# Transposes, Gram products and a running maximum, reordered in the opening of a one-core language-model block

## The reference

```
h = rms_norm(rms_norm(emb[x], nw) @ projT, None)            # 2 x 1024 x 512
h = h + attention(layernorm(h), wq, wk, wv, wo)             # causal softmax(q k' / 4) v
h = h + (silu(n @ w_gate.T) * (n @ w_up.T)) @ w_down.T      # n = layernorm(h)
```

## Time and profile before

| | |
|---|---|
| median of 3 executions | 723.34 us (723.07 to 725.62) |
| the profiled execution | 722.81 us |
| its span, first to last instruction | 721.0 us |
| instructions | 16350 |
| TensorE busy | 693.3 us (96%) |
| VectorE busy | 414.4 us (57%) |
| ScalarE busy | 334.5 us (46%) |
| GpSimd busy | 295.6 us (41%) |

### The profile page before, as it was taken

The page is one execution under the profiler, slowest core; times in us unless marked ns, Lnnn a source line. Parts: engine busy times, 40 slices in busy tenths (PEclk is TensorE's granted clock), DMA queues, the critical chain, the costliest instruction groups (busy, mean ns, idle before and its releaser), DMA issues.

```text
span 721.0 us, 16350 instructions
## 1 busy us (share of the span) xinstructions
PE 693.3 (96%) x6399; PEld 530.2 (74%) x6399; DVE 414.4 (57%) x1041; ACT 334.5 (46%) x691; POOL 295.6 (41%) x398
## 2 busy tenths in 40 slices
PE   8459989999999999999999999999999999999998
PEld 5359679974898569965997489856996499847873
DVE  7867789885654556554655465555655365543320
ACT  6426368862565226631665046622674066512320
POOL 5020212241365426752565436642665246611220
PEclk9859999999999999999999999999999999999999
DMA  8759410011000110002000210012000300000000
GB/s 319 306 196 401 150 40 2 2 28 63 33 2 1 61 61 2 2 17 97 9 2 2 69 54 3 1 47 76 2 2 1 107 15 2 1 16 15 2 1 29
DMA packets 10459, 40.37 MB, mean 56 GB/s; under 512 B 1808, under 2 KB 2576, under 8 KB 8592
## 3 DMA queue, kind: packets, MB, share of 16 engines
q1 hardware_dynamic: 6912, 25.44, 9.1%
q0 software_dynamic: 3328, 13.11, 5.7%
q10 hardware_dynamic: 144, 0.79, 0.3%
HBM read 29.89 MB, written 9.44 MB: 55 GB/s over the span
## 4 chain that ended last, share of the span: by engine, by line
PE 88%; DVE 8%; ACT 2%; issue 1%; POOL 1%; DVEq 0%; POOLq 0%; ACTq 0%
PE banks L1106 15%; PE banks L1108 15%; PE banks L1107 15%; PE banks L1197 6%; PE banks L1199 6%; PE banks L1198 6%; PE banks L1060 4%; PE banks L1078 3%; PE banks L1049 2%; PE banks L1142 2%; PE banks L1144 2%; PE banks L1143 2%; PE banks L1084 1%; PE banks L1038 1%; PE banks L1085 1%
## 5 line engine op out<-in xcount | busy, mean ns | idle before, releaser
L1108 PE MATMUL banks<-xnT_and_h,ffn_weights 128*128 128x256 f16 x1024 | 279.0, 272 | 0.0
L1106 PE MATMUL banks<-xnT_and_h,ffn_weights 128*128 128x256 f16 x1024 | 278.8, 272 | 0.1
L1107 PE MATMUL banks<-xnT_and_h,ffn_weights 128*128 128x256 f16 x1024 | 278.9, 272 | 0.0
L374 POOL TENSOR_TENSOR gated_split<-gate_work,gated_split 128x256 f16<-128x256 f32 x128 | 86.7, 678 | 260.6 <-ACT gated_split L518 260.6
L378 POOL TENSOR_TENSOR weights_split<-weights,weights_split 128x512 f16<-128x512 f32 x96 | 111.3, 1159 | 0.0
L1106 PEld LDWEIGHTS banks<-xnT_and_h,ffn_weights 128*128 128x128 f16 x1024 | 101.0, 99 | 11.9 <-DVE xnT_and_h L878 0.6
L1108 PEld LDWEIGHTS banks<-xnT_and_h,ffn_weights 128*128 128x128 f16 x1024 | 100.0, 98 | 11.8
L1107 PEld LDWEIGHTS banks<-xnT_and_h,ffn_weights 128*128 128x128 f16 x1024 | 99.9, 98 | 11.2
L506 ACT ACTIVATE gate_work<-banks,scales 128x256 f32<-128x256 f32 x128 | 60.7, 474 | 99.8 <-PE banks L1108 99.7
L828 DVE SCALAR_TENSOR_TENSOR weights<-weights,counts_T 128x512 f32<-128x512 f32 x128 | 87.8, 686 | 11.6 <-ACT weights L514 11.5
L514 ACT ACTIVATE weights<-banks,scales 128x512 f32<-128x512 f32 x128 | 87.3, 682 | 14.5 <-PE banks L1060 14.5
(11 more groups left out here) (232 smaller groups left out, 1063.9 us busy)
## 6 DMA issues: line engine op xcount, KB each, us to landing
ffn_weights<-in_ffn_w SPq DMA_DIRECT2D x12, 1024.0 KB, 11.2
out_rows_dram<-ffn_weights SPq DMA_DIRECT2D x16, 256.0 KB, 2.0
xnT_and_h<-in_wqkv SPq DMA_DIRECT2D x1, 1536.0 KB, 8.6
local_table<-gated_split SPq DMA_DIRECT2D x2, 640.0 KB, 4.4
local_table<-xnT_and_h SPq DMA_DIRECT2D x2, 640.0 KB, 6.0
gated_split<-in_projT SPq DMA_DIRECT2D x4, 256.0 KB, 4.0
ffn_weights<-in_wo SPq DMA_DIRECT2D x1, 1024.0 KB, 10.6
token_table<-weights_split ACTq DMA_DIRECT2D x1, 768.0 KB, 5.2
```

The lines of the kernel that those rows point to most:

```text
L374: g.tensor_tensor(gtl[:, j, :], g2[j % 2], gth[:, j, :], ALU.subtract).then_inc(gt_lo, 1)
L1106: t.matmul(o, wh, xTh[m % 2][:, c, :], start=c == 0, stop=False)
L1107: t.matmul(o, wh, xTl[m % 2][:, c, :], start=False, stop=False)
L1108: last = t.matmul(o, wl, xTh[m % 2][:, c, :], start=False, stop=c == DC - 1)
```

## The change

- VectorE computes the indices and ranks ahead of the QKV scales, and the permutation ahead of the low part of Q.
- TensorE makes the key tables ahead of the transposes of K.
- Each key table is copied out in two halves of 512 columns, the first by ScalarE, the second by VectorE. ScalarE waits for `kn` first, then copies its two halves and KstA; VectorE copies KstB after its own halves.
- The prefix over the eight groups is made by doubling: a memset and three maxima, then one, then one more, with a scratch tile of 256 columns. For sequence 1 it moves from slots 0 to 7 into slots 3 to 5.
- Of the Gram products six come before `turn(0)` and six after it, where 16 came before it; 14 are in slot 0 (20 before), 12 in slot 1, and nine in each of slots 2 to 11 (eight before).

```diff
-GU_LEAD = 16
-GU_GRAM = {0: (16, 36), 1: (36, 48), **{s: (32 + 8 * s, 40 + 8 * s) for s in range(2, 12)}}
+GU_LEAD = (6, 12)
+GU_GRAM = {0: (12, 26), 1: (26, 38), **{s: (20 + 9 * s, 29 + 9 * s) for s in range(2, 12)}}
-GROUP_SLOTS = range(0, 8)
+GROUP_SLOTS = range(3, 6)
...
+        gtwo = agth[:, 5 * BLK:6 * BLK]
...
             actq.wait_ge(tab["kn"], 1)
+            for b in range(B):
+                actq.wait_ge(tab["kb"], b + 1)
+                a.activation(Kb[b][:, 0:512], bank[2 - 2 * b], ACT.Copy).then_inc(tab["kb_ev_act"], 1)
             a.activation(KstA[0:64, :], bank16[5][0:64, :], ACT.Copy).then_inc(tab["kn_ev"], 1)
-            actq.wait_ge(tab["kn_ev"], 1)
-            a.activation(KstB[64:128, :], bank16[5][64:128, :], ACT.Copy).then_inc(tab["kn_ev"], 1)
...
-            dve.wait_ge(tab["qkv_sum"], 1)
-            root_powers(POWQ, bank[2][:, 0:3], 3)
-            link(v.tensor_scalar(sc[:, 8:11], sc[:, 60:63], QKV_UP, None, ALU.mult))
-            v.tensor_scalar(sc[:, 16:19], sc[:, 8:11], st[:, 24:25], None, ALU.mult).then_inc(tab["cols"], 1)
-            v.tensor_scalar(c_exp, pw(POWQ), pw(POWQ + 1), 0.25 / QKV_UP ** 2, ALU.mult, ALU.mult)
...
             link(v.tensor_reduce(t_rank, t_cmp.rearrange("p (b u) -> p b u", b=B), AX.X, ALU.add))
+            dve.wait_ge(tab["qkv_sum"], 1)
+            root_powers(POWQ, bank[2][:, 0:3], 3)
+            link(v.tensor_scalar(sc[:, 8:11], sc[:, 60:63], QKV_UP, None, ALU.mult))
+            v.tensor_scalar(sc[:, 16:19], sc[:, 8:11], st[:, 24:25], None, ALU.mult).then_inc(tab["cols"], 1)
+            v.tensor_scalar(c_exp, pw(POWQ), pw(POWQ + 1), 0.25 / QKV_UP ** 2, ALU.mult, ALU.mult)
+
+            for b in range(B):
+                v.tensor_scalar(t_perm[:, b * P:(b + 1) * P], t_iota_r, t_rank[:, b:b + 1], None, ALU.is_equal).then_inc(tab["perm"], 1)
+
             qt = t_q.rearrange("p (h c d) -> p h c d", h=HEADS, d=HD)
             q3 = bank[7].rearrange("p (h d) -> p h d", d=HD)
             dve.wait_ge(tab["qh"], 1)
             v.scalar_tensor_tensor(qt[:, :, 2, :], q3, r_q, qt[:, :, 0, :], ALU.mult, ALU.subtract).then_inc(tab["qlow"], 1)
-            for b in range(B):
-                v.tensor_scalar(t_perm[:, b * P:(b + 1) * P], t_iota_r, t_rank[:, b:b + 1], None, ALU.is_equal).then_inc(tab["perm"], 1)
...
-            def key_table(b):
-                o = (1 - b) * 1024
-                dve.wait_ge(tab["kb"], b + 1)
-                v.tensor_copy(Kb[b], ps[:, o:o + 1024]).then_inc(tab["kb_ev"], 1)
-
             dve.wait_ge(tab["qT"], 2)
             v.tensor_copy(t_QT[:, 1024:2048], bank16[7]).then_inc(tab["qT_ev"], 1)
-            key_table(0)
-            key_table(1)
+            for b in range(B):
+                dve.wait_ge(tab["kb"], b + 1)
+                v.tensor_copy(Kb[b][:, 512:1024], bank[3 - 2 * b]).then_inc(tab["kb_ev"], 1)
+            dve.wait_ge(tab["kn"], 1)
+            dve.wait_ge(tab["zeroed"], 4)
+            v.tensor_copy(KstB[64:128, :], bank16[5][64:128, :]).then_inc(tab["kn_ev"], 1)
...
-            def group_step(j, b=1):
+            def group_step(i, b=1):
                 G = gpre[b].rearrange("p (j h) -> p j h", j=8)
-                if j == 0:
-                    v.memset(G[:, 0, :], NEG).then_inc(tab["gstep"], 1)
+                top = (L0, L1)[b].rearrange("p (i j h) -> p i j h", i=16, j=8)[:, 15]
+                X = gtwo.rearrange("p (j h) -> p j h", j=8)
+                if i == 0:
+                    dve.wait_ge(tab["scan"], 16 * b + 16)
+                    v.memset(G[:, 0, :], NEG)
+                    for first in (G, X):
+                        v.tensor_tensor(first[:, 1:3, :], top[:, 0:2, :], top[:, 0:1, :].broadcast_to([P, 2, HEADS]), ALU.max)
+                    v.tensor_tensor(X[:, 3:8, :], top[:, 2:7, :], top[:, 1:6, :], ALU.max).then_inc(tab["gstep"], 1)
+                elif i == 1:
+                    dve.wait_ge(tab["gstep"], 2 * b + 1)
+                    v.tensor_tensor(G[:, 3:8, :], X[:, 3:8, :], X[:, 1:6, :], ALU.max).then_inc(tab["gstep"], 1)
                 else:
-                    L = (L0, L1)[b].rearrange("p (i j h) -> p i j h", i=16, j=8)
-                    dve.wait_ge(tab["scan"], 16 * b + 16)
-                    dve.wait_ge(tab["gstep"], 7 * b + j)
-                    v.tensor_tensor(G[:, j, :], G[:, j - 1, :], L[:, 15, j - 1, :],
-                                    ALU.max).then_inc(tab["gstep"] if j < 7 else tab["groups"], 1)
+                    dve.wait_ge(tab["gstep"], 2 * b + 2)
+                    v.tensor_tensor(G[:, 5:8, :], G[:, 5:8, :], G[:, 1:4, :], ALU.max).then_inc(tab["groups"], 1)
...
-            for j in range(8):
-                group_step(j, 0)
+            for i in range(3):
+                group_step(i, 0)
...
-            pe.wait_ge(tab["kl"], 1)
-            for g in range(KV):
-                for a in range(2):
-                    last = t.transpose(bank16[5][a * STK:(a + 1) * STK, g * P:(g + 1) * P], t_kst[:, g * STK:(g + 1) * STK], id16[:, :])
-            last.then_inc(tab["kn"], 1)
...
+            pe.wait_ge(tab["kl"], 1)
             pe.wait_ge(tab["perm"], 2)
             pe.wait_ge(tab["cols"], 1)
             pe.wait_ge(tab["vl"], 1)
             key_tables(0)
             pe.wait_ge(tab["index"], 1)
             key_tables(1)
+            for g in range(KV):
+                for a in range(2):
+                    last = t.transpose(bank16[5][a * STK:(a + 1) * STK, g * P:(g + 1) * P], t_kst[:, g * STK:(g + 1) * STK], id16[:, :])
+            last.then_inc(tab["kn"], 1)
...
             pe.wait_ge(tab["kb_ev"], 1)
+            pe.wait_ge(tab["kb_ev_act"], 1)
             pe.wait_ge(tab["qT_ev"], 2)
             score_banks(0, (2, 6, 3, 7))
             pe.wait_ge(tab["h0"], 1)
             pe.wait_ge(tab["kb_ev"], 2)
+            pe.wait_ge(tab["kb_ev_act"], 2)
             score_banks(0, (0, 4))
             pe.wait_ge(tab["kn_ev"], 2)
             score_banks(0, (1, 5)).then_inc(tab["s_tab"], 1)
...
-            gate_up_gram(0, GU_LEAD)
...
+            gate_up_gram(0, GU_LEAD[0])
             turn(0)
+            gate_up_gram(*GU_LEAD)
             phase(0, True, False, 0)
```

More of the change, by code:

```diff
@@ L216, in lm_block @@
             "wo_hi", "wo_lo", "nseen", "diag",
-            "key", "perm", "seen_mm", "index", "kn", "kn_ev", "kb", "kb_ev", "qT", "qT_ev", "s_tab", "scan", "groups",
+            "key", "perm", "seen_mm", "index", "kn", "kn_ev", "kb", "kb_ev", "kb_ev_act", "qT", "qT_ev", "s_tab", "scan", "groups",
             "filler", "onsum", "vf", "gu_gram", "gu_diag", "gu_sum", "gu_scaled", "gstep", "gram", "dn_diag", "dn_sum", "dn_max", "dn_scaled")}
```

## The result

| | before | changed |
|---|---|---|
| median of 20 executions each | 724.45 us (723.07 to 725.84) | 722.94 us (722.14 to 723.65) |
| the profiled execution | 722.81 us, span 721.0 | 722.60 us, span 720.9 |

The ratio of the times is 0.9978 (95% interval 0.9972 to 0.9984), so the change saves 1.5 us or 0.2%, within the half per cent that was called no difference. The two profiled executions differ by only 0.2 us.

A forecast was written before the change was run, and what follows sets the result against it. The bound was how soon TensorE reaches its steady part, decided in the first 93 us. Gains of 0.06 + 0.23 + 0.3 made 0.6 us, taking the median 723.34 to 722.7; range 722.2 to 723.2, chance 0.52.

The forecast's parts named there:

- the sum: Whole forecast gain before the first gate product: 0.06 between the scans, 0.23 for the stall, 0.3 for later waits; 0.6 us.
- Up to the first scan: Opening: ScalarE's half tables queue behind its wait for the K transposes, so the scan stays near 28.41; no change.
- Between the scans: Group steps end sooner, at about 37.2, but TensorE's second scores decide the second scan's start; gain 0.06 us.
- After the scans: Turn comes 1.1 us sooner, six Gram products fill the 0.46 us stall before score 0, later waits shrink; 0.23 plus 0.3.
- later waits: TensorE's weight loads waiting 0.19 and 0.23 us for the stacked query; first goes, about 0.1 of the second stays; gain 0.3.
- gained is the stall, at half clock, as long as the clock still rises at 50.5: Before score 0: filling TensorE's 0.46 us of idle time at half clock gains 0.23 us of full-speed work.
- theory W: Forecast's own account: Gram products cover the half-clock hole before score 0 and two stacked-query waits; 0.55 us faster.
- 1: Rival, whole front: every edit pays what it removes, 1.1 before the first scan, 0.6, 1.1; -2.8 us, 720.5; chance 0.12.
- 2: Rival, opening: idle around the key tables lowers TensorE's clock before 28 us, scan +1.0; 723.8, up to 724.5; chance 0.16.
- 3: Rival, after the scans: without the hole TensorE's clock rises up to 2 us sooner; -1.0 us, 721.7; chance 0.10.
- 4: Rival, after the scans: TensorE's clock rises up to 2 us later; +1.0 us, 723.7; chance 0.06.

The follow-up runs named there:

- Gram edit alone: Kernel before with only the Gram products rearranged: 6 before turn 0, 6 behind it, then 14, 12 and nine a slot; 722.72 us, ratio 0.9983.
- wait behind: Changed kernel with ScalarE's wait for the K transposes moved behind its two half tables; 722.19 us, on another chip 721.87 us; ratios to before 0.9980 and 0.9981.
- first set: Runs on one chip of one part of the change at a time on the kernel before, plus the moved ScalarE wait; kernel before there 723.98 us.
- front alone: Kernel before with only the opening's edits (VectorE's order, key tables ahead of the K transposes, copies in halves); 724.10 us, ratio 1.0004.
- groups alone: Kernel before with only the group prefix made by doubling; 724.35 us, ratio 1.0007.
- third set: Runs on another chip: kernel before with late ScalarE copy 724.72 us; changed kernel 723.03, with ScalarE's wait moved 721.87, that plus ten products behind the turn 722.44.

## Why the prediction was right, and where its size was off

The forecast was 722.7 and the time is 722.94, but that the two are so close is partly luck. The step from before is 1.5 us where I had 0.6. And I took the 0.6 from 723.34, the median of three executions; the 20 of the comparison have theirs at 724.45, from which 0.6 less is 723.85, outside the range that I called the forecast. The baseline was 1.1 too low and the gain 0.9 too small, and the two errors nearly cancel. The profile of the changed kernel bears out the steps of the sum, with one that was mis-sized.

**Up to the first scan: right.** By this profile's clock less 0.21, which is the clock of before: the query transposes end at 23.3 (23.3 forecast), the tables start at 24.24 (24.25), and ScalarE starts its half tables at 25.81 (25.8), having waited 1.53 (1.3). The scan starts 0.12 sooner where I had no change: in the chain the two halves and KstA took 0.60, 0.49 and 0.91, 2.00 in all for my 2.22. The wait in ScalarE's queue costs 0.86, shown by moving it. That VectorE and ScalarE pass no instruction that waits is what the Trainium skill (TensorE: Matmul & The Clock Gate, Architectural detail) states, and this trace agrees: VectorE copies its half of the first table from 25.13, while ScalarE stands idle until the K transposes end at about 26.0.

**Between the scans: right.** Group maxima done 0.7 ahead of the scores (0.5 forecast), the scans 0.04 closer together instead of 0.06, nothing to measure when done alone.

**After the scans: the mechanism right, its size by one execution.** By the chain the turn comes at 46.18 by the clock of before (46.25 forecast), there is no hole before score 0, and both later waits are gone. At the gate product the three profiles of the changed kernel are 0.40, 0.26 and 0.23 ahead of the two of before, less than 0.6. In these the clock came back 0.2, 0.5 and 0.6 later than in the profile shown; with half of that added, an estimate, they are 0.51, 0.53 and 0.53 ahead, which is near the sum. The 0.3 for the later waits is the less certain part: where the clock was back early (Gram edit alone, wait behind, 30.6 to 31.9), two such waits stand in the trace, 0.41 to 0.54 and 0.17.

The step of the sum that was mis-sized is "gained is the stall, at half clock, as long as the clock still rises at 50.5". It priced the hole of the one execution that I had. What the runs showed in its place: the moment at which the clock comes back differs between executions of one kernel, and in part of those of the kernel before the low stretch is 3.4 us longer, 23.9 instead of 20.5. The three profiles with 23.9 have score 0 late by 0.6 to 1.1 us, and the gate product 1.3 to 2.0 us later. On the first set's chip 12 of 33 executions of the kernel before are of this kind, and their median is 1.1 us above that of the 20 at 0.986. The changed kernel's 20 executions all have a mean clock of 0.985 or 0.986.

How far this is shown. A hole of 1.6 us, made on purpose, gave the long low stretch in ten of ten executions and cost 1.5 us. On the first set's chip the mean clocks show it in 25 of 54 executions of the three kernels without products behind the turn (before, front alone, groups alone) and in none of 21 with them (Gram edit alone, wait behind). There it explains about half of the 1.2 us. That it is behind the 1.5 us of the result too is argued: 14 of those 20 executions of before took over 724 us, but their clocks are not on record. On the other two chips the kernel before shows none in 75 executions, and the difference between the kernels was 0.65 (0.1 by the medians) and 0.3 us, about theory W's share or less. Which part of the Gram edit takes it away, the earlier turn or the six products behind it, is open: both came together on the one chip where it occurred. What makes ScalarE's copy late in those executions is open as well: its other inputs were there, and no run took it apart.

Of the rivals, 1 fell with the queue order (0.86 of its 1.1 in the opening was there to be had, by another edit), and 2 did not occur (clock full until 30.4). 3 and 4 were the right question: the clock came back anywhere from 30.6 to 37.3 behind the diagonal step, and how often it comes late counts in a median, which one profile can't tell.

## What to carry to other kernels

Where a copy is split between two engines, look at what stands ahead of it in each queue: a wait left in front of the new instruction took back 0.86 us here, and one moved line recovered it. When work is moved from one place of a busy engine's queue to another, only the idle time that it then fills is gained (0.46 us here), not the time by which one step comes sooner (1.1). And a single profile need not be of the usual kind of execution: lay its own time beside a list of many times before pricing a stall by it, and take the baseline from more than three.

## What the runs showed of the hardware

- The granted clock was low for 17.1, 20.5 or 23.9 us and nothing between, in fourteen profiles. One kernel can have different ones: the kernel before 20.5 in two profiles, and by its mean clocks 23.9 in 12 of 33 executions on one chip.
- The fall to half came 0.1 us (Gram edit alone) to 3.5 us (wait behind) behind the start of the first scan, where TensorE has just gone idle; the moment of the return moves with it.
- In the profiles with a hole of 0.48 us before score 0 the clock was back at 32.6 to 33.4 behind the diagonal step, in those with 1.07, 1.49 and 1.58 at 36.0 to 37.3, and in those without a hole at 30.6 to 34.0.
- An earlier return is not all gained: with the wait behind, the clock was back about 3 us sooner and the scans were 0.9 sooner, but the gate product came 1.1 to 1.3 sooner (74.37 against 75.50 to 75.67), with TensorE waiting for the stacked query. Of the 11 executions in the third set four have the short low stretch (0.988), and they are no faster: median 721.91 against 721.67 of the other seven.
- The same write of the last local piece, issued at 35.6 us in both, landed at 39.5 us in one profile and at 41.8 in another, and GpSimd fetched at 40.2 and at 42.6, with the first scan at 28.30 us in both (Gram edit alone, groups alone).
